# Head mixing with rows of exponentials sorted by DMA and 64x64 products

## The chip, the cores and the metric

The kernel runs on one core of a Trainium2 chip. The time is the device time of one execution, in microseconds (us). One core has five engines that run their own queues in order and meet at semaphores: TensorE (PE in the profile; PEld is its loading of weights), VectorE (DVE), ScalarE (ACT), GpSimd (POOL) and SyncE (SP), which here issues DMAs.

## The reference, cut to what matters

The program is a whole network (a convolution stage, fast-weight attention, a pattern layer, this attention, a layer of experts). The change is in the attention with mixed heads; there are 4 images of 1024 positions, 8 heads of 32 channels:

```python
attn = jnp.einsum('bhnd,bhmd->bhnm', q, k) * scale
attn = jax.nn.softmax(attn, axis=-1)
attn = jnp.einsum('gh,bhnm->bgnm', conv_w, attn) + conv_b[None, :, None, None]
mean = attn.mean(axis=(0, 2, 3), keepdims=True)
var = attn.var(axis=(0, 2, 3), keepdims=True)
attn = (attn - mean) * jax.lax.rsqrt(var + BN_EPS)
attn = attn * bn_gamma[None, :, None, None] + bn_beta[None, :, None, None]
out = jnp.einsum('bhnm,bhmd->bhnd', attn, v)
```

So for each query the 8 rows of probabilities (one per head, 1024 keys long) are replaced by 8 mixtures of them, whose sum and sum of squares over everything give the normalization, and the mixtures weigh the values.

## The kernel before, in words

`head_mixing_stage` works image by image (`b`, 4 of them). After the projections of an image (`project`, `value_sums`) it goes through 64 tiles of 16 queries. A tile is [128, 1024] float32: its 128 rows are 8 heads times 16 queries, its columns the keys. 8 tiles make a block (128 queries); `t` is a tile's place in its block and `u` the tile's parity, which picks one of two buffers. In the order of a tile's life:

- POOL `masked(i)` makes the masked queries `qd` of tile i; PE `scores(i)` multiplies them with the keys, as 8 products of 64 rows by 32 columns that run side by side, into two banks of PSUM (one pair of banks per parity).
- DVE `maxima(i)` takes the negative maximum of each row; ACT `exponentials(i)` writes `ex` to SBUF and the row sums; DVE `inverse(i)` inverts the sums; POOL `weights(i)` multiplies the constant `kron` (the mixing matrix spread over 16 queries) by the inverses, which gives the weights `mix`.
- PE `mixed(i)` multiplies `mix` (128 by 128) with the tile, two products of 512 columns, into banks 4 and 5. ACT `keep(i)` copies them to `Aq`, ACT `squares(i)` sums the squares, DVE `running(i)` sums the values.
- PE `turn(i)` transposes `Aq` in 8 pieces into banks 6 and 7, and DVE `evacuate(i)` copies these to `A`.
- Once per block PE `values` multiplies `A` with the values (64 products) into banks 6 and 7, and DVE `outputs` copies the result to `H`.

Nothing but the order in which the code is written decides the order on an engine. On PE a tile is `mixed(i)`, `turn(i-1)`, `scores(i+2)`; at t = 1 `values` stands between `mixed` and `scores`, and `turn` comes last. On DVE it is `maxima(i+1)`, `running(i-1)`, `inverse(i+1)`, `outputs` at t = 1, `evacuate(i-1)`. On ACT it is `squares(i-1)`, `exponentials(i+1)`, `keep(i)`. Before `mixed(i)` PE waits for the masked queries of tile i+2, for `exponentials(i)`, for the weights of tile i and for `keep(i-1)`. SP issues seven loads when the stage begins and nothing more in it.

Of the kernel before, what the change touches and what calls it, by code (L numbers as in the profile page):

```python
# [12 lines left out]
ALU = mybir.AluOpType  # L13
# [1638 lines left out]
def head_mixing_stage(k, H):  # L1652


    nc, d = k.nc, k.d
# [7 lines left out]
    with ExitStack() as ctx:  # L1663
# [6 lines left out]
        kron = sb("kron", [P, HEADS, QT_])  # L1670
# [4 lines left out]
        ex = sb("ex", [P, 2, HW])  # L1675
        nm = sb("nm", [P, 2]); rsum = sb("rsum", [P, 2]); rinv = sb("rinv", [P, 2])
        mix = sb("mix", [P, 2, HEADS * QT_])
# [10 lines left out]
        names = ("w kron hb q q_act q_dve k k_ev v v_ev vs vs_ev qd s nm ex rinv mix aq cp sq run t ac pv pv_ev "  # L1688
                 "tot var sd dch pch").split()
        (s_w, s_kron, s_hb, s_q, s_q_act, s_q_dve, s_k, s_k_ev, s_v, s_v_ev, s_vs, s_vs_ev, s_qd, s_s, s_nm, s_ex, s_rinv,  # L1690
         s_mix, s_aq, s_cp, s_sq, s_run, s_t, s_ac, s_pv, s_pv_ev, s_tot, s_var, s_sd, s_dch, s_pch) = (
# [4 lines left out]
        with nc.Block() as block:  # L1696
            @block.sync
            def _(sp):
                sp.dma_start(wq[:, :, :, :], d["hm_wq"]).then_inc(s_w, 16)
                sp.dma_start(w[:, :, :], d["hm_w"]).then_inc(s_w, 16)  # L1700
                sp.dma_start(wcol[:, :], d["hm_wcol"]).then_inc(s_w, 16)
                sp.dma_start(wrow[:, :, :], d["hm_wrow"]).then_inc(s_w, 16)
                sp.dma_start(qmask[:, :, :], d["hm_qmask"]).then_inc(s_w, 16)
                sp.dma_start(cbcol[:, :], d["hm_cbcol"]).then_inc(s_w, 16)
                sp.dma_start(lane[:, :, :], d["hm_lane"]).then_inc(s_w, 16)

            @block.gpsimd
            def _(pool):
                def masked(b, i, u):
                    pool.wait_ge(s_s, b * TI + i + 1)  # L1710
                    src = q[:, :, bass.ds(i * QT_, QT_)].unsqueeze(2).broadcast_to([P, NPAIR, 2, QT_])
                    pool.tensor_tensor(qd[:, u, :, :, :], src,  # L1712
                                       qmask[:, :, :].unsqueeze(1).broadcast_to([P, NPAIR, 2, QT_]),
                                       ALU.mult).then_inc(s_qd, 1)

                def weights(b, i, u):
                    pool.wait_ge(s_rinv, b * TI + i + 1)
                    pool.tensor_tensor(mix[:, u, :], kron[:, :, :].rearrange("p g n -> p (g n)"),  # L1718
                                       rinv[:, u:u + 1].broadcast_to([P, HEADS * QT_]), ALU.mult).then_inc(s_mix, 1)

                pool.wait_ge(s_w, 112)
                pool.wait_ge(s_kron, 1)
                k.credit(pool, s_s, 2)
                with pool.Fori(0, B) as b:
                    pool.wait_ge(s_v, b + 1)
                    pool.tensor_copy(hb[:, :, :], H[:, :, bass.ds(b * HW, HW)]).then_inc(s_hb, 1)
                    pool.wait_ge(s_q_act, b * 4 + 4)
                    pool.wait_ge(s_q_dve, b * 4 + 4)
                    masked(b, 0, 0)
                    masked(b, 1, 1)  # L1730
                    with pool.Fori(0, TI // 2 - 1) as j:
                        for u in range(2):
                            masked(b, j * 2 + u + 2, u)
                            weights(b, j * 2 + u, u)
                    for u in range(2):
                        weights(b, TI - 2 + u, u)

            @block.tensor
            def _(pe):
# [4 lines left out]
                with pe.Fori(0, B) as b:  # L1744
# [69 lines left out]
                    def values(n):  # L1814
                        pe.wait_ge(s_ac, b * TI + n * NQ + NQ)
                        for m in range(MT):
                            for o in range(CH):
                                for j in range(4):
                                    g = 4 * o + j
                                    mm = pe.matmul(bank[6 + o][32 * j:32 * j + 32, 0:QB], v[:, m, DH * g:DH * g + DH],  # L1820
                                                   A[:, m, g, :], start=(m == 0), stop=(m == MT - 1))
                        mm.then_inc(s_pv, 1)

                    def block_of_queries(n, first, last):

                        for t in range(NQ):
                            i = n * NQ + t
                            more = not (last and t >= NQ - 2)
                            mixed(i, t % 2, more)
                            if t == 0 and not first:  # L1830
                                turn(i - 1, 1)
                            if t == 1 and not first:
                                values(n - 1)
                            if t > 1:
                                turn(i - 1, (t - 1) % 2)
                            if more:
                                scores(i + 2, t % 2)
# [8 lines left out]
                    value_sums()  # L1846
                    block_of_queries(0, True, False)
# [13 lines left out]
            def _(act):  # L1861
                k.load_table(act, ACT.Exp)
                with act.Fori(0, B) as b:

                    def exponentials(i, u):
                        act.wait_ge(s_nm, b * TI + i + 1)
                        act.activation(ex[:, u, :], flat2(psum[:, 2 * u:2 * u + 2, :]), ACT.Exp,  # L1867
                                       bias=nm[:, u:u + 1], accum_out=rsum[:, u:u + 1]).then_inc(s_ex, 1)
# [22 lines left out]
                    keep(0, 0, fresh=True)  # L1891
                    squares(0, 0)
                    act.wait_ge(s_aq, b * TI + 1)
                    exponentials(2, 0)
                    keep(1, 1, fresh=True)
                    with act.Fori(1, TI // 2 - 1) as j:
                        for u in range(2):
                            i = j * 2 + u
                            squares(i - 1, 1 - u)
                            act.wait_ge(s_aq, b * TI + i)  # L1900
                            exponentials(i + 1, 1 - u)
                            keep(i, u)
                    squares(TI - 3, 1)
                    act.wait_ge(s_aq, b * TI + TI - 2)
                    exponentials(TI - 1, 1)
                    keep(TI - 2, 0)
                    squares(TI - 2, 0)
                    keep(TI - 1, 1)
# [5 lines left out]
            def _(dve):  # L1914
                own = Steps(dve, s_pch)
                dve.wait_ge(s_w, 112)
                dve.tensor_tensor(kron[:, :, :], k.const("mkron").rearrange("p (g n) -> p g n", g=HEADS),
                                  wcol[:, :].unsqueeze(2).broadcast_to([P, HEADS, QT_]), ALU.mult).then_inc(s_kron, 1)
                dve.memset(sums[:, :], 0.0).then_inc(s_run, 1)
                dve.wait_ge(s_run, 1)  # L1920
                with dve.Fori(0, B) as b:
# [28 lines left out]
                    def block_of_queries(n, first, last):  # L1950
                        for t in range(NQ):
                            i = n * NQ + t
                            more = not (last and t == NQ - 1)
# [4 lines left out]
                            if more:  # L1958
# [14 lines left out]
                    maxima(0, 0)  # L1973
                    dve.wait_ge(s_vs, b + 1)
# [466 lines left out]
def constants():  # L2441
# [9 lines left out]
        "mkron": (i % 16) == (j % 16),  # L2451
# [9 lines left out]
def layout(inputs):  # L2461
# [54 lines left out]
    out["hm_wcol"] = np.repeat(a["L3_attn_conv_w"].T, P // HEADS, 0)  # L2516
    out["hm_wrow"] = np.repeat(a["L3_attn_conv_w"], DH, 0).reshape(CH, P, HEADS).transpose(1, 0, 2)
    out["hm_qmask"] = np.repeat((np.arange(P)[:, None, None] % 64 // DH == np.arange(2)[None, :, None]), 16, 2).astype(np.float32)
    out["hm_cbcol"] = np.repeat(a["L3_attn_conv_b"], P // HEADS)[:, None]
    mine = np.arange(P)[:, None, None] // 16 == np.arange(CH)[None, :, None] * 4 + np.arange(P)[None, None, :] // DH  # L2520
# [28 lines left out]
```

## Time and profile before

| | |
|---|---|
| median of 3 runs | 4664.12 us (4653.84 to 4673.27) |
| the profiled execution, its own time | 4656.92 us |
| its span (first to last instruction) | 4654.9 us |
| busy share of the span | PE 84%, DVE 60%, ACT 47%, POOL 18% |
| the stage of the change, first to last mixing product | 2801.3 to 4064.1 us |

Busy shares are means over stages with different limits; what is asked of this profile is what one tile of the stage waits for. Starts in the rows are us from the span's start. The ends of matmuls are modelled, so where one operation follows another the distance of the starts is the safer number.

### The profile page before, as it was taken

To read this page: it belongs to the slowest core of one execution; us is meant where nothing else is said; L and a number is where in the kernel's file an instruction comes from. 1 tells how busy PE (TensorE), PEld (TensorE's weight loads), DVE (VectorE), ACT (ScalarE), POOL (GpSimd) and SP (SyncE) were. 2 spreads that over 40 slices of the span, in tenths; PEclk is the share of its full clock that TensorE was granted. 3 is DMA by queue.
4 is the path that set the end of the run, shared out by engine and by line. 5 is a ranking of instruction groups with operands and counts; after the bars stand their busy time and mean duration, and the time that the engine had idled before them with its cause. 6 is when DMAs were issued, how large, how long until landed. Compare 5 with 4: busy or idle time off the path is not lost. (4 is left out here: it accounts for less than half of the span.)

```text
span 4654.9 us, 156020 instructions
## 1 busy us (share of the span) xinstructions
PE 3895.6 (84%) x64268; PEld 2373.9 (51%) x64269; DVE 2777.9 (60%) x5395; ACT 2194.1 (47%) x4155; POOL 820.1 (18%) x2119
## 2 busy tenths in 40 slices
PE   3468999879789997678889659999999999975995
PEld 1236777534367775245555434544545445544763
DVE  3545666320356663578888648858858858843343
ACT  1124555221345552366666517747747747712221
POOL 0000000000000000255555401111111111105022
PEclk7779999889899998899999879999999999977997
DMA  1001111000011110100000000000000000025223
GB/s 49 0 17 43 48 50 50 25 18 0 15 44 48 51 48 24 44 1 1 1 1 1 0 11 1 0 1 1 0 1 0 0 1 0 1 88 190 65 90 103
DMA packets 84139, 131.60 MB, mean 28 GB/s; under 512 B 11216, under 2 KB 66800, under 8 KB 82928
## 3 DMA queue, kind: packets, MB, share of 16 engines
q1 hardware_dynamic: 77808, 112.19, 7.2%
q0 software_dynamic: 6144, 16.79, 1.1%
q8 instruction: 134, 2.20, 0.2%
q14 instruction: 53, 0.43, 0.0%
HBM read 70.21 MB, written 58.72 MB: 28 GB/s over the span
## 5 line engine op out<-in xcount | busy, mean ns | idle before, releaser
L1801 PE MATMUL psum<-hm_ex,hm_mix 128*128 128x512 f32 x1024 | 510.7, 622 | 42.1 <-ACT hm_Aq L1881 38.1
L1867 ACT ACTIVATE hm_ex<-psum,hm_nm 128x1024 f32<-128x1024 f32 x256 | 285.6, 1116 | 298.5 <-DVE hm_nm L1925 298.5
L1801 PEld LDWEIGHTS psum<-hm_ex,hm_mix 128*128 128x128 f32 x1024 | 175.6, 191 | 352.6 <-issue 344.9
L1940 DVE COPY hm_A<-psum 128x1024 f32<-128x1024 f32 x256 | 313.0, 1222 | 51.1 <-PE psum L1810 47.8
L1935 DVE TENSOR_SCALAR_CACHE_REDUCE hm_plus<-hm_Aq,hm_cbcol,hm_sums 128x1024 f32<-128x1024 f32 x256 | 340.6, 1331 | 0.0
L1925 DVE TENSOR_REDUCE hm_nm<-psum 128x1 f32<-128x1024 f32 x256 | 311.2, 1216 | 14.0 <-PE psum L1789 14.0
L1810 PEld LDWEIGHTS psum<-K,hm_Aq 128*128 128x128 f32 x2048 | 236.7, 140 | 150.0 <-issue 145.4
L1872 ACT ACTIVATE hm_junk<-hm_Aq 128x1024 f32<-128x1024 f32 x256 | 270.6, 1057 | 30.3
L1347 ACT ACTIVATE pt_signs<-pt_acts,pt_tb 128x1024 f32<-128x1024 f32 (+1 forms) x224 | 227.6, 1017 | 115.5 <-POOL pt_tb L1214 94.8
L1789 PE MATMUL psum<-hm_kt,hm_qd 64*32 64x512 f32 x4096 | 280.4, 606 | 0.0
L1810 PE MATMUL psum<-K,hm_Aq 128*128 128x128 f32 x2048 | 266.6, 273 | 5.7 <-DVE hm_A L1940 5.6
L1881 ACT ACTIVATE hm_Aq<-psum 128x1024 f32<-128x1024 f32 x256 | 259.7, 1014 | 11.3 <-PE psum L1801 11.3
L1261 PE MATMUL psum<-pt_w_proc,pt_keptT 128*128 128x512 f32 x512 | 226.8, 601 | 10.0 <-ACT pt_keptT L1332 10.0
L690 PE MATMUL psum<-fw_w,fw_stage 128*128 128x512 f32 (+1 forms) x512 | 211.6, 538 | 24.5 <-DMA fw_w<-in_slow 24.4
L2252 ACT ACTIVATE ex_ht<-psum,ex_b 128x128 f32<-128x128 f32 x320 | 91.5, 368 | 286.7 <-PE psum L2184 286.7
L1718 POOL TENSOR_TENSOR hm_mix<-hm_kron,hm_rinv 128x128 f32<-128x128 f32 x256 | 102.2, 399 | 664.4 <-DVE hm_rinv L1930 664.4
L1431 DVE TENSOR_SCALAR_CACHE_REDUCE pt_over<-pt_acts,pt_tb 128x1024 f32<-128x1024 f32 (+1 forms) x96 | 101.8, 1098 | 166.7 <-POOL pt_tb L1214 166.7
L1241 PE MATMUL psum<-K,pt_acts 128*128 128x128 f32 x640 | 101.5, 321 | 106.1 <-DVE pt_acts L1459 80.1
L1712 POOL TENSOR_TENSOR hm_qd<-hm_q,hm_qmask 128x128 f32<-128x128 f32 x256 | 116.1, 454 | 411.9 <-PE psum L1789 300.7
L670 POOL TENSOR_TENSOR fw_loff<-fw_bg,K 128x256 f32<-128x256 f32 x64 | 55.0, 860 | 675.6 <-DVEq L983 675.6
L1261 PEld LDWEIGHTS psum<-pt_w_proc,pt_keptT 128*128 128x128 f32 x512 | 97.6, 193 | 129.4 <-issue 129.4
L723 PE MATMUL psum<-fw_rk,fw_ntx 64*64 64x64 f32 x4096 | 155.2, 227 | 5.5 <-issue 4.9
(370 smaller groups left out, 7996.7 us busy)
## 6 DMA issues: line engine op xcount, KB each, us to landing
fw_late<-fw_away SPq DMA_DIRECT2D x64, 384.0 KB, 3.1
ex_rows_in<-ex_zero SPq DMA_DIRECT2D x2, 5120.0 KB, 24.5
ex_xs<-ex_rows_in SPq DMA_DIRECT2D x80, 128.0 KB, 2.0
ex_rows_out<-ex_ys SPq DMA_DIRECT2D x80, 128.0 KB, 1.7
fw_away<-fw_kk SPq DMA_DIRECT2D x64, 128.0 KB, 1.7
fw_away<-fw_tr SPq DMA_DIRECT2D x64, 128.0 KB, 1.7
fw_away<-fw_qm SPq DMA_DIRECT2D x64, 128.0 KB, 1.7
ex_w<-in_ex_w SPq DMA_DIRECT2D x2, 4096.0 KB, 22.2
```

Source lines behind the costliest of these rows:

```text
L690: mm = pe.matmul(bank[n][:, 0:hi - lo], stage[:, h, :], w[:, h, lo:hi], start=(h == 0), stop=(h == CH - 1))
L1261: mm = pe.matmul(bank[4 + u], keptT[:, c, u, :], w_proc[:, c, :], start=(c == 0), stop=(c == N_IN // P - 1))
L1347: act.activation(signs[:, u, 0:n], acts[:, lane(j), u, 0:n], ACT.Sign, bias=tb[:, lane(j), u, 0:1], accum_out=tb[:, lane(j), u, 1:2]).then ...
L1789: mm = pe.matmul(bank[2 * u + c][32 * pr:32 * pr + 32, :], qd[64 * c:64 * c + 64, u, pr, :, :].rearrange("p j n -> p (j n)"), kt[64 * c:64 ...
L1801: mm = pe.matmul(bank[4 + c], mix[:, u, :], ex[:, u, 512 * c:512 * c + 512], start=True, stop=True)
L1810: mm = pe.transpose(bank[6 + m // 4][:, P * (m % 4):P * (m % 4) + P], Aq[:, u, P * m:P * m + P], k.const("ident"))
L1867: act.activation(ex[:, u, :], flat2(psum[:, 2 * u:2 * u + 2, :]), ACT.Exp, bias=nm[:, u:u + 1], accum_out=rsum[:, u:u + 1]).then_inc(s_ex, 1)
L1872: act.activation(junk[:, :], Aq[:, u, :], ACT.Square, accum_out=ssq[:, bass.ds(b * TI + i, 1)]).then_inc(s_sq, 1)
L1881: act.activation(Aq[:, u, :], flat2(psum[:, 4:6, :]), ACT.Copy).then_inc(s_cp, 1)
L1925: dve.tensor_reduce(nm[:, u:u + 1], flat2(psum[:, 2 * u:2 * u + 2, :]), AX.X, ALU.max, negate=True).then_inc(s_nm, 1)
L1935: dve.tensor_scalar(plus[:, :], Aq[:, u, :], cbcol[:, :], sums[:, :], ALU.add, ALU.add, accum_out=sums[:, :]).then_inc(s_run, 1)
L1940: dve.tensor_copy(A[:, :, :, QT_ * t:QT_ * t + QT_], flat2(psum[:, 6:8, :]).rearrange("p (m g n) -> p m g n", m=MT, g=HEADS)).then_inc(s_a ...
```

## The change

Each tile of exponentials gets a second copy, `sorted`, whose rows are in another order. Row 16h+n of `ex` is head h, query n. SP waits for `exponentials(i)` and issues two DMAs from SBUF to SBUF: even rows of `ex` to partitions 0 to 63 of `sorted`, odd rows to 64 to 127. A row is 1025 elements long (4100 bytes), since the row sum is written behind the 1024 exponentials and travels with them. Now each half of the partitions holds 8 heads times 8 queries, no product crosses the halves, and `mixed` is four products of 64 rows by 64 columns by 512 instead of two of 128 by 128 by 512. `kron` and `mix` shrink to 64 columns. The output rows now mean another pair of head and query, so `evacuate`, `outputs` and `values` read and write in other patterns (the same numbers of instructions and elements), and constants are laid out anew.

The order around it moves too: scores are made three tiles ahead instead of two, maxima two ahead instead of one, and exponentials two ahead, behind `keep` instead of ahead of it. `inverse(i)` waits for the two DMAs of tile i.

```diff
-        ex = sb("ex", [P, 2, HW])
+        ex = sb("ex", [P, 2, PITCH]); sorted_ = sb("sorted", [P, 2, PITCH])
...
+                with sp.Fori(0, B * TI // 2) as j:
+                    for u in range(2):
+                        sp.wait_ge(s_ex, j * 2 + u + 1)
+                        for r in range(2):
+                            sp.dma_start(sorted_[64 * r:64 * r + 64, u, 0:HW + 1], ex[r:P:2, u, 0:HW + 1]
+                                         ).then_inc((s_mv0, s_mv1)[u], 16)
...
                         if more:
-                            pe.wait_ge(s_qd, b * TI + i + 3)
-                            pe.wait_ge(s_ex, b * TI + i + 1)
+                            pe.wait_ge(s_qd, b * TI + i + 4)
+                            pe.wait_ge(s_ex, b * TI + i + 2)
                         pe.wait_ge(s_mix, b * TI + i + 1)
                         pe.wait_ge(s_cp, b * TI + i + 1)
+                        pe.sem_inc(s_go, 1)
                         for c in range(2):
-                            mm = pe.matmul(bank[4 + c], mix[:, u, :], ex[:, u, 512 * c:512 * c + 512],
-                                           start=True, stop=True)
+                            for r in range(2):
+                                o = slice(64 * r, 64 * r + 64)
+                                mm = pe.matmul(bank[4 + r][64 * c:64 * c + 64, :], mix[o, u, :],
+                                               sorted_[o, u, 512 * c:512 * c + 512], start=True, stop=True)
...
-                                scores(i + 2, t % 2)
+                                scores(i + 3, (t + 1) % 2)
...
                     def inverse(i, u):
-                        dve.wait_ge(s_ex, b * TI + i + 1)
-                        dve.reciprocal(rinv[:, u:u + 1], rsum[:, u:u + 1]).then_inc(s_rinv, 1)
+                        dve.wait_ge((s_mv0, s_mv1)[u], b * (TI * 16) + (i * 16 + (32 - 16 * u)))
+                        dve.reciprocal(rinv[:, u:u + 1], sorted_[:, u, HW:HW + 1]).then_inc(s_rinv, 1)
...
-                        dve.tensor_copy(A[:, :, :, QT_ * t:QT_ * t + QT_],
-                                        flat2(psum[:, 6:8, :]).rearrange("p (m g n) -> p m g n", m=MT, g=HEADS)
-                                        ).then_inc(s_ac, 1)
+                        dve.tensor_copy(A[:, :, :, QT_ * t:QT_ * t + QT_].rearrange("p m g (r n) -> p r (m g) n", r=2),
+                                        psum[:, 6:8, :].rearrange("p r (a n) -> p r a n", n=HQ)).then_inc(s_ac, 1)
...
-                            if more:
-                                maxima(i + 1, (t + 1) % 2)
+                            if not (last and t >= NQ - 2):
+                                maxima(i + 2, t % 2)
```

On POOL, in the loop over pairs of tiles, the masked queries (`hm_qd`) of a tile stood ahead of the weights (`hm_mix`) for which the same product of PE waits. The loop before:

```order
L1731 ISA
L1712 ISA
L1712 TENSOR_TENSOR hm_qd<-hm_q,hm_qmask 128x128
L1717 ISA
L1718 TENSOR_TENSOR hm_mix<-hm_kron,hm_rinv 128x128
```

The same loop of the change:

```order
L1742 ISA
L1728 TENSOR_TENSOR hm_mix<-hm_kron,hm_rinv 128x64
L1720 ISA
L1722 ISA
L1722 TENSOR_TENSOR hm_qd<-hm_q,hm_qmask 128x128
```

The two have changed places: `weights(i)` comes first and is half as wide, `masked(i+3)` follows it, and `mixed(i)` waits for both.

On ACT, in the loop over pairs of tiles (`hm_junk` is `squares`, `hm_ex` the exponentials, `hm_Aq` is `keep`), before:

```order
L1872 ACTIVATE hm_junk,hm_ssq<-hm_Aq 128x1024
L1900 REGISTER_ALU
L1866 ISA
L1867 ACTIVATE hm_ex,hm_rsum<-psum,hm_nm 128x1024
L1876 REGISTER_ALU
L1878 REGISTER_ALU
L1881 ACTIVATE hm_Aq<-psum 128x1024
```

and in the change:

```order
L1892 ACTIVATE hm_junk,hm_ssq<-hm_Aq 128x1024
L1896 ISA
L1898 REGISTER_ALU
L1901 ACTIVATE hm_Aq<-psum 128x1024
L1886 ISA
L1887 ACTIVATE hm_ex<-psum,hm_nm 128x1024
```

`keep(i)` moved ahead of the exponentials, which now belong to tile i+2. On SP two DMAs per tile are new, after the stage's loads:

```order
L1710 ISA
L1714 DMA hm_sorted<-hm_ex 64x1025 x2
L1712 REGISTER_ALU
L1714 DMA hm_sorted<-hm_ex 64x1025 x2
L1710 REGISTER_ALU
```

That is a pair of tiles per turn of the loop, with nothing between the two DMAs of a tile.

## Rows read from the trace of the kernel before

**Rows 1.** The page, its first line.

```profile
span 4654.9 us, 156020 instructions
```

**Rows 2.** Windows, 100 us inside the stage: busy us per engine, granted clock.

```profile
3300.00:3400.00 100.00, 96.76 (x1022) 50.25 (x1021) 86.29 (x121) 73.91 (x114) 19.18 (x45) 1.00 0.00 0
```

**Rows 3.** Groups of the stage by line: busy, mean ns, idle before and releaser.

```profile
L1801 PE MATMUL psum<-hm_ex,hm_mix 128*128 128x512 f32 x1024 | 510.7, 622 | 42.1 <-ACT hm_Aq L1881 38.1 <-POOL hm_mix L1718 4.0
L1867 ACT ACTIVATE hm_ex<-psum,hm_nm 128x1024 f32<-128x1024 f32 x256 | 285.6, 1116 | 298.5 <-DVE hm_nm L1925 298.5
```

**Rows 4.** Timeline, one ordinary tile: start, duration, engine, line, operation.

```profile
3336.51 1.98 PE L1801 MATMUL psum<-hm_ex,hm_mix 128*128 128x512 f32 x4
...
3337.99 1.12 ACT L1867 ACTIVATE hm_ex<-psum,hm_nm 128x1024 f32<-128x1024 f32 x1 [0.42 <-DVE hm_nm L1925]
3338.34 1.04 PE L1810 MATMUL psum<-K,hm_Aq 128*128 128x128 f32 x8
...
3339.01 0.19 ACT L1867 ACTIVATION_READ_ACCUMULATOR hm_ex<-psum,hm_nm 128x1 f32 x1
3339.10 1.01 ACT L1881 ACTIVATE hm_Aq<-psum 128x1024 f32<-128x1024 f32 x1
...
3339.23 0.16 DVE L1930 RECIPROCAL hm_rinv<-hm_rsum 128x1 f32<-128x1 f32 x1
...
3339.30 1.09 PE L1789 MATMUL psum<-hm_kt,hm_qd 64*32 64x512 f32 x16
...
3339.47 0.40 POOL L1718 TENSOR_TENSOR hm_mix<-hm_kron,hm_rinv 128x128 f32<-128x128 f32 x1 [2.17 <-DVE hm_rinv L1930]
...
3340.32 1.98 PE L1801 MATMUL psum<-hm_ex,hm_mix 128*128 128x512 f32 x4
...
3340.65 0.45 POOL L1712 TENSOR_TENSOR hm_qd<-hm_q,hm_qmask 128x128 f32<-128x128 f32 x1 [0.78 <-PE psum L1789]
```

**Rows 5.** Timeline behind the values of a block.

```profile
3350.01 0.49 DVE L1947 COPY H<-psum 128x128 f32 x2 [3.00 <-PE psum L1820]
...
3351.84 1.22 DVE L1940 COPY hm_A<-psum 128x1024 f32<-128x1024 f32 x1 [1.34 <-PE psum L1810]
...
3352.98 1.21 DVE L1925 TENSOR_REDUCE hm_nm<-psum 128x1 f32<-128x1024 f32 x1
...
3355.34 1.01 ACT L1881 ACTIVATE hm_Aq<-psum 128x1024 f32<-128x1024 f32 x1
...
3355.71 0.40 POOL L1718 TENSOR_TENSOR hm_mix<-hm_kron,hm_rinv 128x128 f32<-128x128 f32 x1 [4.24 <-DVE hm_rinv L1930]
3356.23 0.45 POOL L1712 TENSOR_TENSOR hm_qd<-hm_q,hm_qmask 128x128 f32<-128x128 f32 x1
...
3356.49 1.96 PE L1801 MATMUL psum<-hm_ex,hm_mix 128*128 128x512 f32 x4 [1.08 <-ACT hm_Aq L1881]
3356.67 1.21 DVE L1925 TENSOR_REDUCE hm_nm<-psum 128x1 f32<-128x1024 f32 x1
```

**Rows 6.** Timeline of PE, the same place one block earlier.

```profile
3321.32 1.96 PE L1801 MATMUL psum<-hm_ex,hm_mix 128*128 128x512 f32 x4 [1.08 <-ACT hm_Aq L1881]
```

**Rows 7.** Timeline of SP, the stage's first two loads.

```profile
2753.75 0.33 SPq L1699 DMA_DIRECT2D hm_wq<-in_hm_wq  x1
2754.13 0.59 SPq L1700 DMA_DIRECT2D hm_w<-in_hm_w  x1
```

**Rows 8.** DMA issues: count, KB each, median us from issue to landing.

```profile
ex_xs<-ex_rows_in SPq DMA_DIRECT2D x80, 128.0 KB, 2.0
...
fw_away<-fw_tr SPq DMA_DIRECT2D x64, 128.0 KB, 1.7
...
hm_wq<-in_hm_wq SPq DMA_DIRECT2D x1, 512.0 KB, 3.8
hm_w<-in_hm_w SPq DMA_DIRECT2D x1, 512.0 KB, 4.1
...
ho_w<-in_hm_out SPq DMA_DIRECT2D x1, 256.0 KB, 2.6
```

More of the change, by code:

```diff
@@ L1687, in head_mixing_stage @@
         st = sb("st", [P, 8, CH]); toff = sb("toff", [P, CH, B])
[L1688 to L1691, printed above, removed]
+        names = ("w kron hb q q_act q_dve k k_ev v v_ev vs vs_ev qd s nm ex mv0 mv1 rinv mix aq cp sq run t ac pv pv_ev "
+                 "tot var sd go dch pch").split()
+        (s_w, s_kron, s_hb, s_q, s_q_act, s_q_dve, s_k, s_k_ev, s_v, s_v_ev, s_vs, s_vs_ev, s_qd, s_s, s_nm, s_ex, s_mv0, s_mv1, s_rinv,
+         s_mix, s_aq, s_cp, s_sq, s_run, s_t, s_ac, s_pv, s_pv_ev, s_tot, s_var, s_sd, s_go, s_dch, s_pch) = (
              k.sem(f"s_hm_{n}") for n in names)
@@ L1730, in _ @@
                     masked(b, 1, 1)
-                    with pool.Fori(0, TI // 2 - 1) as j:
+                    masked(b, 2, 0)
+                    with pool.Fori(0, TI // 2 - 2) as j:
                         for u in range(2):
-                            masked(b, j * 2 + u + 2, u)
                             weights(b, j * 2 + u, u)
-                    for u in range(2):
-                        weights(b, TI - 2 + u, u)
+                            masked(b, j * 2 + u + 3, 1 - u)
+                    weights(b, TI - 4, 0)
+                    masked(b, TI - 1, 1)
+                    for i in range(TI - 3, TI):
+                        weights(b, i, i % 2)
             @block.tensor
@@ L1827, in block_of_queries @@
                             i = n * NQ + t
-                            more = not (last and t >= NQ - 2)
+                            more = not (last and t >= NQ - 3)
                             mixed(i, t % 2, more)
@@ L1846, in _ @@
                     value_sums()
+                    pe.wait_ge(s_qd, b * TI + 3)
+                    pe.wait_ge(s_ex, b * TI + 1)
+                    pe.sem_inc(s_go, 1)
+                    scores(2, 0)
                     block_of_queries(0, True, False)
@@ L1891, in _ @@
                     keep(0, 0, fresh=True)
+                    exponentials(2, 0)
                     squares(0, 0)
-                    act.wait_ge(s_aq, b * TI + 1)
-                    exponentials(2, 0)
                     keep(1, 1, fresh=True)
+                    exponentials(3, 1)
                     with act.Fori(1, TI // 2 - 1) as j:
@@ L1899, in _ @@
                             squares(i - 1, 1 - u)
-                            act.wait_ge(s_aq, b * TI + i)
-                            exponentials(i + 1, 1 - u)
                             keep(i, u)
[L1903 to L1908, printed above, removed]
+                            exponentials(i + 2, u)
+                    for u in range(2):
+                        squares(TI - 3 + u, 1 - u)
+                        keep(TI - 2 + u, u)
                     squares(TI - 1, 1)
@@ L1952, in block_of_queries @@
                             i = n * NQ + t
-                            more = not (last and t == NQ - 1)
-                            if more:
-                                maxima(i + 1, (t + 1) % 2)
+                            if not (last and t >= NQ - 2):
+                                maxima(i + 2, t % 2)
                             if not (first and t == 0):
                                 running(i - 1, (t - 1) % 2)
-                            if more:
+                            if not (last and t == NQ - 1):
                                 inverse(i + 1, (t + 1) % 2)
@@ L1973, in _ @@
                     maxima(0, 0)
+                    maxima(1, 1)
                     dve.wait_ge(s_vs, b + 1)
@@ L2450, in constants @@
         "gn_avg": same(8) / 8.0,
-        "mkron": (i % 16) == (j % 16),
+        "mkron": (i % 8) == (j % 8),
         "one": np.ones((P, P)),
@@ L2515, in layout @@
     out["hm_wq"] = np.repeat(rows(a["L3_attn_w_qkv"][:, :C]).reshape(P, CH, 4, 1, 64), 2, 3).reshape(P, CH, 4, P)
[L2516 removed]
+    out["hm_wcol"] = np.tile(np.repeat(a["L3_attn_conv_w"].T, 8, 0), (2, 1))
     out["hm_wrow"] = np.repeat(a["L3_attn_conv_w"], DH, 0).reshape(CH, P, HEADS).transpose(1, 0, 2)
     out["hm_qmask"] = np.repeat((np.arange(P)[:, None, None] % 64 // DH == np.arange(2)[None, :, None]), 16, 2).astype(np.float32)
[L2519 to L2520 removed]
+    out["hm_cbcol"] = np.tile(np.repeat(a["L3_attn_conv_b"], 8), 2)[:, None]
+    mine = np.arange(P)[:, None, None] // 8 % 8 == np.arange(CH)[None, :, None] * 4 + np.arange(P)[None, None, :] // DH
     out["hm_lane"] = mine.astype(np.float32)
```

23 lines of the change are left out of this document (12 added, 11 removed).

## The prediction

> **What bounds the kernel now.** I read the page first for the size of things: 4654.9 us in all [rows 1]. Then the windows inside the stage: in 100 us PE is busy 96.76, DVE 86.29, ACT 73.91, at a granted clock of 1.00, the upper of its two levels, 2.4 GHz [rows 2]. That looks like a stage bound by PE, and the groups agree: the mixing products, which the change halves, are PE's largest item with 510.7 us and waited only 42.1 us, while ACT stands idle 298.5 us for DVE's maxima [rows 3].
>
> A mean over 100 us mixes two things, so I went on to the timeline. In an ordinary tile PE starts its product at 3336.51, the transposes at 3338.34, the scores at 3339.30 and the next product at 3340.32: 1.83 + 0.96 + 1.02 = 3.81 us, with no gap [rows 4]. But DVE is hardly less full. Where it does not wait for PE, its five instructions of a tile (maxima, sum of values and the reading of its sum, inverse, evacuation) take from 3352.98 to 3356.67, 3.69 us [rows 5]. So an ordinary tile has 0.12 us to give, whatever PE saves, and two tiles cannot take less than 7.38 us against 7.62 now.
>
> The rest is at the block's values. The same product, with the same wait of 1.08 us, starts at 3321.32 and at 3356.49 [rows 5, 6], so a block takes 35.17 us: six ordinary steps of 3.81 and two that hold the values, 35.17 - 22.86 = 12.31 us. There DVE waits 3.00 us for the values and 1.34 us for the transposes behind them [rows 5].
>
> **The change, part by part.** *The product.* Nothing before is 64 by 64 by 512. The nearest row is the scores: eight 64-row products of 512 columns side by side, 1.02 us from their start to the next operation's [rows 4]. I take 1.02 for the four new ones instead of 1.83: PE saves 0.81 us per tile. Bounds: 0.91 (half of 1.83) and 1.83 (no two side by side).
>
> *What this buys at the best.* On ordinary steps 0.12 us each, DVE's limit. At the values the product of tile t = 1 stands ahead of them on PE and everything behind follows it, so the two steps shrink by its 0.81.
>
> *What is new on the path.* Between exponentials and inverse there are now two DMAs, and each tile's product leads to the exponentials of the tile two later: `mixed(i)`, `keep(i)`, `exponentials(i+2)`, the DMAs, `inverse(i+2)`, `weights(i+2)`, `masked(i+5)` behind it on POOL, `mixed(i+2)`. This ring must close once in two tiles. Term by term, with L for the time from SP's first issue to the second landing:
> - product to the start of `keep`: 1.09, and 0.26 more by which POOL's start lies behind the modelled end of the scores (3340.65 against 3340.39) [rows 4]: 1.35. With the 0.03 by which DVE follows ACT it would be 1.12.
> - `keep` to `exponentials`, which stand right behind it: 1.01 less the overlap of 0.10 seen between ACT's neighbours (3339.01 + 0.19 against 3339.10) [rows 4]: 0.92.
> - exponentials to the read sum, 3337.99 to 3339.20: 1.21. To SP, 0.03 (DVE starts 0.03 after it) [rows 4].
> - landing to DVE 0.03; inverse to POOL's start, 3339.23 to 3339.47: 0.24 [rows 4].
> - weights: 0.40 for 128 columns [rows 4], 0.20 for 64; I take it as proportional (bounds 0.20 and 0.40).
> - masked queries: 0.45, and the 0.12 between 3356.11 and 3356.23 [rows 5]: 0.57. They stood ahead of the weights before, where they cost this path nothing.
> - POOL to PE: 0.14, as from `keep`'s end, 3356.35, to the product at 3356.49 [rows 5].
>
> The sum is 4.69 + L for two tiles. Before, no ring through a DMA existed. It is free if it is under 7.38, that is L under 2.69, and costs what PE's saving gave on ordinary steps at L = 2.93.
>
> *L.* No row shows a copy from SBUF to SBUF, so I bound it. The two DMAs move 128 x 4100 bytes = 524.8 kB (512.5 KB). The second issue starts 0.38 us behind the first [rows 7], while the first is still on its way. Low end: 256 KB land in 2.6 us, and the 1024 KB of the first two loads in 0.38 + 4.1 = 4.48 [rows 7, 8]; so 786 kB more took 1.88 us, 418 kB per us. 128 KB out of SBUF land in 1.7 [rows 8], of which 131/418 = 0.31 are the bytes, 1.39 the rest. 1.39 + 524.8/418 = 2.65. High end: 4.1 + 0.38 = 4.48, the second of two loads in a queue. The nearest row is the load of 512 KB in 128 rows of 4096 bytes, 3.8 us; it reads memory, and at 128 KB a copy that ends in SBUF (2.0) is 0.3 slower than one that starts there (1.7) [rows 8]. I take 3.8 - 0.3 = **3.5**.
>
> *What is queued behind the new wait.* On DVE `inverse(i+1)` waits for the landing, and `outputs`, `evacuate(i-1)` and the next `maxima` stand behind it. PE's transposes and ACT's exponentials wait for those. On SP nothing else is queued. What costs nothing: the other patterns of `evacuate` and `outputs` (same elements; if the pieces of 8 made a copy slower, it would show on DVE at once), 0.81 us less of PE (it turns into waiting).
>
> *The sum, per image* (63 steps between 64 products: three at the start, two at each of 7 sets of values, 46 ordinary ones, or 23 pairs):
> - pairs at 4.69 + 3.5 = 8.19 instead of 7.62: 0.57 each. The last two have no masked queries to wait for, 7.62, so 0. 21 x 0.57 = +12.0.
> - values: 7 x -0.81 = -5.7.
> - filling: the first product of an image comes later by L and by the masked queries less the narrower weights, 3.5 + 0.57 - 0.20 = +3.9.
> - the last product is shorter: -0.8.
>
> +9.4 per image, x 4 = **+38 us**. The profiled execution had 4656.92 us, of which 4654.9 is span; it would have 4695. The median of the runs is 7.2 us above it, 0.15%, and I put the sum on that: 4664 + 38 = **4702 us**. With other L the same sum is 4 x (21 x (L - 2.93) + 2 x (L - 3.50) + L + 0.37 - 6.5): zero at L = 3.1, and 24 x 4 = 96 us for each us of L. The bound of 0.5%, 23 us, about what a measurement can tell from no change here, lies at L = 2.9 and 3.35.
>
> **The rivals.** *The DMAs are hidden* (ends faster). At L = 2.65 the ring takes 7.34, under DVE's 7.38: 23 pairs x -0.24 - 5.7 + 3.0 - 0.8 = -9.0, x 4 = -36 us, 4628. For it: the transfer's bytes need 1.26 us at the rate of rows 7 and 8, no memory is read, and no other DMA runs (the windows show a share of 0.00 [rows 2]). Against: no row of 512 KB landed under 3.8. It decides below L = 2.9.
>
> *Half rate.* Each DMA writes 64 partitions only. If that halves the rate, the bytes take 2 x 1.26 = 2.51 and L = 3.90: pairs 8.59, 21 x 0.97 + 2 x 0.40 - 5.7 + 4.3 - 0.8 = 19.0, x 4 = +76 us, 4740. No row shows a copy into 64 partitions, so the traces speak neither for nor against; it lies between my bounds. The Trainium skill has this as a rule (SBUF — State Buffer, "Door 1: The DMA port swizzle" and "Can I just issue two DMAs to hit both halves?"): 64 partitions reach 8 of 16 ports, a copy into them was measured at 196 GB/s, and two copies to the two halves serialize. By that figure, an estimate, the bytes take 2.68 us, L is 4.07 and the time 4757; no run here shows it yet.
>
> *No net change.* L between 2.9 and 3.35 gives back on 46 steps what the 7 sets of values save.
>
> *PE is not faster.* If the four products run one pair after the other (1.83), 0.81 comes back on the ring and at the values: (21 + 2) x 0.81 + 5.7 = 24 us per image, +134 with the forecast, 4798. The scores, which do run side by side, speak against it. A clock that falls to 1.2 GHz because PE now waits would cost in the same way; the windows show 1.00 at 96.76 busy of 100 [rows 2], and nothing of a stage with PE at 3.0 of 4.1.
>
> **How the numbers follow.** The forecast, L from 3.35 to 3.7, 0.28; half rate, L above that, 0.24; hidden, 0.32; no net change, 0.13; PE not faster, 0.03. So faster by over 0.5% 0.32, within it 0.13, slower 0.55. The low end is the hidden case, 4628, with a little for a product of 0.91: 4625. The high end is near L = 4.48 (21 x 1.55 + 2 x 0.98 - 6.5 + 4.85 = 32.9, x 4 = +131, 4795): 4790. The likeliest case's own range (L 3.35 to 3.9) is 4687 to 4740.
>
> **What the profile after would show.** The DMA issues give L directly: about 3.1 us from the second issue to landing if I am right, 2.3 if hidden, 3.5 or more at half rate. The inverse should be the DVE instruction with the idle time, released by the DMA. Steps between products should alternate in sums of about 8.2 per two tiles with PE idle ahead of the product behind POOL's masked queries or weights; 7.4 with DVE gapless would mean hidden. The product's distance to the next operation should be 1.02. The forecast is wrong if L is under 2.9, if POOL's half-width weights and ACT's order shorten the ring by much more than I took, or if evacuation in pieces of 8 is slower, which would raise DVE's 3.69 itself.

## The result and the profile after

The changed kernel takes 4987.71 us (median of 4 runs, 4977.71 to 4993.21), the kernel before 4663.86 beside it (4 runs). The ratio is 1.0693, with a 95% interval of 1.0668 to 1.0717. The forecast was 4702 and the range ended at 4790: slower was right, but +324 us stand where +38 were predicted.

The profiled execution of the changed kernel, 4977.71 us. First the page: its first line, the four groups that tell most (busy us, mean ns, idle before and releaser), and the DMA issue (KB each, median us to landing).

```profile
span 4975.6 us, 159149 instructions
...
L1817 PE MATMUL psum<-hm_sorted,hm_mix 64*64 64x512 f32 x2048 | 323.8, 704 | 379.8 <-POOL hm_qd L1722 357.0
L1901 ACT ACTIVATE hm_Aq<-psum 128x1024 f32<-128x1024 f32 x256 | 262.4, 1025 | 639.7 <-PE psum L1817 639.7
...
L1956 DVE COPY hm_A<-psum 128x1024 f32<-128x1024 f32 x256 | 309.9, 1211 | 65.9 <-PE psum L1826 65.3
...
L1946 DVE RECIPROCAL hm_rinv<-hm_sorted 128x1 f32<-128x1 f32 x256 | 41.8, 163 | 408.0 <-DMA hm_sorted<-hm_ex 407.6
...
hm_sorted<-hm_ex SPq DMA_DIRECT2D x512, 256.2 KB, 5.3
```

Against [rows 3]: the mixing product shrank from 510.7 to 323.8 us of busy time, but its wait grew from 42.1 to 379.8. On DVE the inverse, an instruction of 0.16 us, waits 408 us for the copies. Evacuation in pieces of 8 costs nothing: 1211 ns, as before (1.22 in [rows 5]).

The windows: 100 us of the stage, as [rows 2], then two neighbouring blocks, each from the first product behind a set of values to the same product one block later, then a block that ran at a granted clock of 1.00 throughout (us; busy us of PE, PEld, DVE, ACT and POOL; granted clock, DMA share, GB/s).

```profile
3300.00:3400.00 100.00, 72.16 (x887) 33.75 (x875) 67.66 (x96) 57.40 (x92) 12.70 (x36) 0.90 0.59 94
3314.97:3358.39 43.42, 30.13 (x385) 14.09 (x385) 29.97 (x42) 25.36 (x40) 5.64 (x16) 0.96 0.61 97
3358.39:3404.96 46.57, 33.89 (x386) 15.72 (x385) 30.27 (x42) 25.36 (x40) 5.64 (x16) 0.85 0.60 92
3860.74:3904.12 43.38, 28.65 (x385) 13.60 (x384) 29.87 (x42) 25.36 (x40) 5.66 (x16) 1.00 0.61 97
```

A block took 35.17 us before. Of the three here two take 43.4 us, and the one with the lowest granted clock takes 46.57. The timeline shows the ring of the prediction closing, once for each parity of tile.

```profile
3404.96 1.09 PE L1817 MATMUL psum<-hm_sorted,hm_mix 64*64 64x512 f32 x8
...
3408.47 0.19 ACT L1887 ACTIVATION_READ_ACCUMULATOR hm_ex<-psum,hm_nm 128x1 f32 x1
...
3409.87 1.09 PE L1817 MATMUL psum<-hm_sorted,hm_mix 64*64 64x512 f32 x8 [1.35 <-POOL hm_qd L1722]
3410.89 1.09 PE L1826 MATMUL psum<-K,hm_Aq 128*128 128x128 f32 x8
...
3411.17 1.02 ACT L1901 ACTIVATE hm_Aq<-psum 128x1024 f32<-128x1024 f32 x1 [1.48 <-PE psum L1817]
...
3412.09 1.11 ACT L1887 ACTIVATE hm_ex<-psum,hm_nm 128x1024 f32<-128x1024 f32 x1
...
3413.09 0.20 ACT L1887 ACTIVATION_READ_ACCUMULATOR hm_ex<-psum,hm_nm 128x1 f32 x1
...
3414.56 0.16 DVE L1946 RECIPROCAL hm_rinv<-hm_sorted 128x1 f32<-128x1 f32 x1 [2.30 <-DMA hm_sorted<-hm_ex]
...
3415.83 1.23 PE L1817 MATMUL psum<-hm_sorted,hm_mix 64*64 64x512 f32 x8 [2.83 <-POOL hm_qd L1722]
3416.99 1.97 PE L1826 MATMUL psum<-K,hm_Aq 128*128 128x128 f32 x8
...
3418.89 1.64 PE L1802 MATMUL psum<-hm_kt,hm_qd 64*32 64x512 f32 x16
3419.18 0.17 DVE L1946 RECIPROCAL hm_rinv<-hm_sorted 128x1 f32<-128x1 f32 x1 [0.96 <-DMA hm_sorted<-hm_ex]
3419.43 0.29 POOL L1728 TENSOR_TENSOR hm_mix<-hm_kron,hm_rinv 128x64 f32<-128x64 f32 x1 [3.92 <-DVE hm_rinv L1946]
3419.68 0.46 POOL L1722 TENSOR_TENSOR hm_qd<-hm_q,hm_qmask 128x128 f32<-128x128 f32 x1
...
3420.47 1.09 PE L1817 MATMUL psum<-hm_sorted,hm_mix 64*64 64x512 f32 x8
```

From 3409.87 the ring runs: product to `keep` 1.30, to the exponentials 0.92, to the read sum 1.20 (3413.29), to the inverse 5.89, to the weights 0.25, to the masked queries 0.25, to the next product but one 0.79: 10.60 us. The other tile's copies take the same: 3408.66 to 3414.56, 5.90. Less 0.03 at each end, **L is 5.84 us**, where 3.5 was taken and 4.48 was the bound. One more thing is in these rows: behind PE's wait of 2.83 the transposes took 1.97 and the scores 1.64, against 1.09 each a tile earlier. There the granted clock is at its lower level, 1.2 GHz (from 3416 to 3420 its mean is 0.58); stretches like this one make the 0.85 of the second block.

### The profile page after: what moved, and what is told of

It is laid out like the page before. It is cut to its first block and busy times, and to the rows that moved or that the text cites. A ratio compares the mean times of both kernels' runs of the same rounds, so it can differ in the third digit from the quotient of the medians.

```text
span 4975.6 us, 159149 instructions
## 1 busy us (share of the span) xinstructions
PE 3859.1 (78%) x65292; PEld 2295.0 (46%) x65293; DVE 2762.4 (56%) x5395; ACT 2169.8 (44%) x4155; POOL 782.4 (16%) x2119
## 5 line engine op out<-in xcount | busy, mean ns | idle before, releaser
L1817 PE MATMUL psum<-hm_sorted,hm_mix 64*64 64x512 f32 x2048 | 323.8, 704 | 379.8 <-POOL hm_qd L1722 357.0
L1901 ACT ACTIVATE hm_Aq<-psum 128x1024 f32<-128x1024 f32 x256 | 262.4, 1025 | 639.7 <-PE psum L1817 639.7
L1826 PEld LDWEIGHTS psum<-K,hm_Aq 128*128 128x128 f32 x2048 | 268.8, 163 | 268.8 <-issue 236.6
L1826 PE MATMUL psum<-K,hm_Aq 128*128 128x128 f32 x2048 | 339.4, 319 | 24.3 <-DVE hm_A L1956 16.5
L1817 PEld LDWEIGHTS psum<-hm_sorted,hm_mix 64*64 64x64 f32 x2048 | 63.6, 145 | 616.0 <-issue 616.0
L1956 DVE COPY hm_A<-psum 128x1024 f32<-128x1024 f32 x256 | 309.9, 1211 | 65.9 <-PE psum L1826 65.3
L1802 PE MATMUL psum<-hm_kt,hm_qd 64*32 64x512 f32 x4096 | 321.3, 691 | 2.6 <-DVE hm_vsum L1990 2.6
L1728 POOL TENSOR_TENSOR hm_mix<-hm_kron,hm_rinv 128x64 f32<-128x64 f32 x256 | 75.4, 295 | 1271.4 <-DVE hm_rinv L1946 1271.4
L1946 DVE RECIPROCAL hm_rinv<-hm_sorted 128x1 f32<-128x1 f32 x256 | 41.8, 163 | 408.0 <-DMA hm_sorted<-hm_ex 407.6
```

The lines of the kernel that those rows point to most:

```text
L1802: mm = pe.matmul(bank[2 * u + c][32 * pr:32 * pr + 32, :], qd[64 * c:64 * c + 64, u, pr, :, :].rearrange("p j n -> p (j n)"), kt[64 * c:64 ...
L1817: mm = pe.matmul(bank[4 + r][64 * c:64 * c + 64, :], mix[o, u, :], sorted_[o, u, 512 * c:512 * c + 512], start=True, stop=True)
L1826: mm = pe.transpose(bank[6 + m // 4][:, P * (m % 4):P * (m % 4) + P], Aq[:, u, P * m:P * m + P], k.const("ident"))
L1901: act.activation(Aq[:, u, :], flat2(psum[:, 4:6, :]), ACT.Copy).then_inc(s_cp, 1)
L1956: dve.tensor_copy(A[:, :, :, QT_ * t:QT_ * t + QT_].rearrange("p m g (r n) -> p r (m g) n", r=2), psum[:, 6:8, :].rearrange("p r (a n) -> ...
```

## The experiments

The theory was that L alone makes the loss, through the ring of 4.69 + L. The rivals were: contention of the copies with the engines, any wait on a DMA, and the clock. All ratios are to the kernel before in the same comparison. The diffs are cut to the lines that matter; `...` marks what is left out of a line.

**The copies by themselves** (`p1_copies`). Eight repetitions of nine kinds of copies, in a stage put ahead of the program, each waited for before the next:

```diff
...
+elif n.startswith("halves"): moves = [(z[64*r:64*r+64, 0:m], a[64*r:64*r+64, 0:m]) for r in range(2)]
+elif n.startswith("alone"):  moves = [(z[0:64, 0:m], a[0:P:2, 0:m])]
+elif n.startswith("spread"): moves = [(z[r:P:2, 0:m], a[64*r:64*r+64, 0:m]) for r in range(2)]
+else:                        moves = [(z[64*r:64*r+64, 0:m], a[r:P:2, 0:m]) for r in range(2)]  # pair
```

> The kernel before with a stage put in ahead, on an idle core, in which SP issues nine kinds of copies from SBUF to SBUF, each kind eight times and each time waiting for it. In the changed kernel the two copies of a tile take 5.87 us from the first issue to the inverse. If that is the price of the copies themselves, the kind `pair` (the same rows, partitions and pitch) takes 5.7 to 5.9 here too; if it comes from sharing SBUF with four busy engines, clearly less, 3.5 to 4.5. If destinations of 64 partitions are what slows them, `one` (all 128 partitions in one copy, in the same order) takes 3.0 to 3.9 and `halves1024` as long as `pair1024`; if rows of 4100 bytes at a pitch of 4112 are, then `pair1024` (4096 bytes, pitch 4096) and `pairwide` (pitch 4352) are faster than `pair`, and `one1024` faster than `one`; if reading every second partition is, `halves1024` is faster than `pair1024`.

The timeline of SP: start, us from the first issue of a kind to the end of its last issue (not to its landing), copies. The sorting pairs of 1025 and of 1024 elements share a row, as do the single copies.

```profile
26.41 90.05 SPq L165 DMA_DIRECT2D pair_to<-pair_from  x32
121.25 42.59 SPq L165 DMA_DIRECT2D pairwide_to<-pairwide_from  x16
168.66 43.68 SPq L165 DMA_DIRECT2D one_to<-one_from  x16
215.18 31.34 SPq L165 DMA_DIRECT2D halves_to<-halves_from  x16
249.74 27.32 SPq L165 DMA_DIRECT2D alone_to<-alone_from  x8
280.43 29.72 SPq L165 DMA_DIRECT2D spread_to<-spread_from  x16
313.12 24.85 SPq L165 DMA_DIRECT2D half_to<-half_from  x16
```

From a kind's first issue to the first of the next kind lie all its repetitions, 16 or 8. So a repetition of the sorting pair takes (121.25 - 26.41) / 16 = 5.93 us, one copy of all 128 partitions 46.52 / 16 = 2.91, two copies of adjacent halves 34.56 / 8 = 4.32, adjacent source into every second partition 32.69 / 8 = 4.09, one copy of every second partition alone (half the bytes) 30.69 / 8 = 3.84. For the sorting pair with half the elements, the last kind, 7 repetitions lie between its first issue and its last two, which take 1.10: (24.85 - 1.10) / 7 = 3.39. So all of L is there on an idle core (5.93 against 5.84), and contention falls. So does the row length: the pair with rows 1088 elements apart took 47.41 / 8 = 5.93, and in the issues view (us from issue to landing) the length in bytes makes no difference:

```profile
pair_to<-pair_from SPq DMA_DIRECT2D x16, 256.2 KB, 4.8
...
one_to<-one_from SPq DMA_DIRECT2D x8, 512.5 KB, 2.9
...
pair_to<-pair_from SPq DMA_DIRECT2D x16, 256.0 KB, 4.8
one_to<-one_from SPq DMA_DIRECT2D x8, 512.0 KB, 2.9
```

Splitting a copy into halves costs 1.4 us, and reading every second partition into 64 adjacent ones costs 1.6 more. Why that reading is slow, these runs do not show.

**No copies** (`e1_no_copy`; the products read the exponentials unsorted, and the inverse waits for the exponentials alone; the result is not the attention's).

```diff
-mm = pe.matmul(..., mix[o, u, :], sorted_[o, u, 512 * c:512 * c + 512], ...)
+mm = pe.matmul(..., mix[o, u, :], ex[o, u, 512 * c:512 * c + 512], ...)
```

> The changed kernel without the copies: the four products read the exponentials where they are, so heads and queries are mixed in the wrong rows, and the inverse waits for the exponentials again. Ring theory (the change lost its time because the ring from one product to the product of the tile two later holds the copies; everything else in it is a gain): the ring is 4.69 us for two tiles, under DVE's 7.38, and the time is about 4628, 0.992 of before. Rival (the loss is on the engines: a clock of 1.2 GHz in part of the stage, evacuations in pieces of 8, four products instead of two): it stays above 4850.

4607.68 us, ratio 0.9868 (0.9845 to 0.9892): the whole loss hangs on the copies, and without them the change would gain 1.3%, 20 us more than the ring theory gave. Rows of PE and ACT show what limits a tile then:

```profile
3305.95 1.09 PE L1811 MATMUL psum<-hm_ex,hm_mix 64*64 64x512 f32 x8 [1.39 <-POOL hm_qd L1716]
...
3307.25 1.03 ACT L1895 ACTIVATE hm_Aq<-psum 128x1024 f32<-128x1024 f32 x1 [1.52 <-PE psum L1811]
...
3308.17 1.11 ACT L1881 ACTIVATE hm_ex<-psum,hm_nm 128x1024 f32<-128x1024 f32 x1
...
3309.17 0.20 ACT L1881 ACTIVATION_READ_ACCUMULATOR hm_ex<-psum,hm_nm 128x1 f32 x1
...
3309.61 0.66 PE L1811 MATMUL psum<-hm_ex,hm_mix 64*64 64x512 f32 x4 [0.53 <-ACT hm_ex L1881]
```

It is a second ring, which the prediction had not seen: product, `keep`, the exponentials two tiles on, and the *next* product, which waits for them ahead of itself: 1.30 + 0.92 + 1.20 + 0.24 = 3.66 us per tile (3305.95 to 3309.61).

**Half the elements** (`e3_half_bytes`; the first 512 columns are not copied, the products read ones there).

```diff
-sp.dma_start(sorted_[64 * r:64 * r + 64, u, 0:HW + 1], ex[r:P:2, u, 0:HW + 1] ...
+sp.dma_start(sorted_[64 * r:64 * r + 64, u, HW // 2:HW + 1], ex[r:P:2, u, HW // 2:HW + 1] ...
```

> The changed kernel with only the second half of each row (and its sum) copied, 513 elements instead of 1025; the products read ones in the first half, so the result is not the attention's. If the copies are bound by their bytes, they take 1.39 + 4.48/2 = 3.6 us, the ring 8.3 and the time about 4715; if by something fixed per copy, they stay above 5 us and the time above 4890.

4705.47 us, ratio 1.0079 (1.0055 to 1.0103). As expected where the cost goes with the bytes: 2.54 us less of L (5.93 to 3.39 on the idle core) gave back 282 us; 244 of them by the formula's 96 us for each us of L, and the clock rose with it (1.00 in the 100 us from 3300).

**One copy of all partitions** (`e4_one_copy`; as many bytes in one copy, unsorted; the result is not the attention's).

```diff
-for r in range(2):
-    sp.dma_start(sorted_[64 * r:64 * r + 64, u, 0:HW + 1], ex[r:P:2, u, 0:HW + 1] ...
+sp.dma_start(sorted_[:, u, 0:HW + 1], ex[:, u, 0:HW + 1] ...
```

> The changed kernel with one copy per tile, all 128 partitions of the exponentials to the same 128 partitions, in place of the two that sort (so the products mix the wrong queries). If the size of L, and in it the reading of every second partition into 64 adjacent ones, makes the loss: one such copy landed 2.9 us after its issue on an idle core, L is 3.2 to 3.5, and by the prediction's formula the time is 4670 to 4705 us. If any DMA in the ring costs this much, or the second wait itself, the time stays above 4900.

4659.44 us, ratio 0.9996 (0.9985 to 1.0007), even a little below what was expected. All the bytes through the ring in one copy cost 1.3% against no copies; the sorting pair costs 8%. So neither the bytes nor a DMA in the ring as such makes the loss. This run changes the number of copies and their pattern together; the copies by themselves part the two, 1.4 us and 1.6.

**Another pattern, same sorting** (`e7_spread4`).

```diff
-for r in range(2):
-    sp.dma_start(sorted_[64 * r:64 * r + 64, u, 0:HW + 1], ex[r:P:2, u, 0:HW + 1] ...
+for r in range(4):
+    sp.dma_start(sorted_[r:P:4, u, 0:HW + 1], ex[32 * r:32 * r + 32, u, 0:HW + 1] ...
```

> The same sorting by four copies of 32 adjacent source partitions each into every fourth partition of the destination, with the masked queries' columns ordered query by query so that the result is the same. If the slow part is the reading of every second partition, L is about 4.5 (three issue distances of 0.5, then a landing of some 2.7, then 0.3 to the inverse) and the time by the formula is 4740 to 4830 us. If any scattering across partitions is as slow as the changed kernel's, or four issues cost more than two, it is 4960 to 5050.

4819.6 us, ratio 1.0344 (1.0323 to 1.0364): half of the loss is gone with four copies instead of two, as expected where the pattern that is read is slow. Its timeline gives the ring a second point:

```profile
3331.62 1.09 PE L1817 MATMUL psum<-hm_sorted,hm_mix 64*64 64x512 f32 x8 [1.65 <-POOL hm_qd L1722]
...
3334.84 0.20 ACT L1887 ACTIVATION_READ_ACCUMULATOR hm_ex<-psum,hm_nm 128x1 f32 x1
...
3339.53 0.16 DVE L1946 RECIPROCAL hm_rinv<-hm_sorted 128x1 f32<-128x1 f32 x1 [1.10 <-DMA hm_sorted<-hm_ex]
...
3340.81 1.09 PE L1817 MATMUL psum<-hm_sorted,hm_mix 64*64 64x512 f32 x8 [1.63 <-POOL hm_qd L1722]
```

From the read sum (3335.04) to the inverse are 4.49 us, so L is 4.43; 4.69 + 4.43 = 9.12, and the pair of tiles takes 9.19.

**Masked queries ahead of the weights** (`e2_mask_first`).

```diff
-weights(b, j * 2 + u, u)
 masked(b, j * 2 + u + 3, 1 - u)
+weights(b, j * 2 + u, u)
```

> The changed kernel with POOL's order of before: the masked queries ahead of the weights for which the same product waits. Ring theory: 0.57 us less in each of about 21 pairs of tiles per image, so 48 us less, 4940. Rival (the masked queries are hidden, the wait on them in the profile is only the last of several that end together): within 0.5% of 4988.

4970.76 us, ratio 1.0642 (1.0616 to 1.0669): 17 us less than the changed kernel, not 48. The product now waits for the weights instead of the masked queries, and the stage ran at the lower clock more often: the product's mean grew from 704 to 747 ns, and the granted clock in the 100 us from 3300 is 0.86 instead of 0.90. That this ate the other 31 us is argued, not shown.

**The clock** (`e8_filler`, `e8b_filler`): products whose result is overwritten, on PE ahead of its wait for the weights; six per tile in the first, one and a half in the second.

```diff
+pe.matmul(bank[4], k.const("ident"), kt[:, 0, :], start=True, stop=True)
+pe.matmul(bank[5][:, 0:256], k.const("ident"), kt[:, 1, 0:256], start=True, stop=True)
 pe.wait_ge(s_mix, b * TI + i + 1)
```

> The changed kernel with six idle products per tile on PE, ahead of the waits for the weights, into the banks that the mixing product then overwrites: PE waits less, the ring is the same. If the 56 us that the ring formula leaves over at L = 5.87 are the clock's (1.2 GHz in parts of the stage), the clock stays near 1.00 and the time is 4915 to 4950 us, though PE does more work. If the rest lies elsewhere in the ring, the time is 4975 to 5030.

5786.73 us, far above both expectations. Such a product takes 0.92 us (half of the 1.83 of the two in [rows 4]), six of them 5.5, more than the wait that they were to fill, so this says nothing of the clock. The second is sized to the wait:

> The changed kernel with one and a half idle products per tile (512 and 256 columns, 1.37 us by the rate of the 128 by 128 product, within the 1.35 to 2.83 us that PE waits) in place of the six that took more than the whole wait. If the 56 us left over by the ring formula at L = 5.87 are the clock's, the granted clock stays near 1.00 in the stage and the time is 4915 to 4950 us. If they lie elsewhere in the ring, it is 4975 to 5030.

4962.31 us, ratio 1.064 (1.0622 to 1.0658). Windows of it, as above:

```profile
3300.00:3400.00 100.00, 90.79 (x944) 42.59 (x940) 68.33 (x96) 57.37 (x91) 12.69 (x36) 1.00 0.62 96
```

With PE kept busy the clock is 1.00, and the kernel is 25 us faster though PE does more. That is less than expected, since the extra products also lengthen a block:

```profile
3362.05:3406.09 44.04, 40.11 (x417) 18.94 (x416) 29.87 (x44) 25.24 (x40) 5.64 (x16) 1.00 0.61 95
```

44.04 us where the changed kernel's block at 1.00 took 43.42 (the mean of four such blocks): 0.62 more, 17 us in the 28 blocks of 4 images. The clock's share in the changed kernel is then about 25 + 17 = 42 us. Its own blocks say nearly the same: the 28 of the profiled execution are together 38 us longer than 28 times 43.42.

**The order alone** (`e6_order_only`): scores three ahead and POOL's new order, with the 128 by 128 products of before and no copies.

> The order part of the change alone: scores three ahead, exponentials and maxima two ahead, POOL's weights ahead of the masked queries, with the mixing products of 128 by 128 and no copies, as before. If the gain of the kernels without a late copy comes from the narrower products, PE's 3.81 us per tile stand here too and the time is 4640 to 4680 us. If the other order alone made that gain, it is 4590 to 4620.

4785.26 us, ratio 1.0256 (1.0239 to 1.0273): both theories fell. The timeline shows the second ring again, now with the wide product:

```profile
3401.68 1.96 PE L1809 MATMUL psum<-hm_ex,hm_mix 128*128 128x512 f32 x4 [0.65 <-ACT hm_ex L1879]
...
3403.82 1.02 ACT L1893 ACTIVATE hm_Aq<-psum 128x1024 f32<-128x1024 f32 x1 [1.35 <-DVE hm_plus L1943]
...
3404.74 1.11 ACT L1879 ACTIVATE hm_ex<-psum,hm_nm 128x1024 f32<-128x1024 f32 x1
...
3406.18 1.96 PE L1809 MATMUL psum<-hm_ex,hm_mix 128*128 128x512 f32 x4 [0.66 <-ACT hm_ex L1879]
```

2.14 + 0.92 + 1.44 = 4.50 us per tile instead of 3.81. (The row of `keep` names DVE, but its start is 0.31 behind the product's 1.83, as it is 0.28 behind the narrow one's 1.02 above: it waits for PE.) The narrow product shortens this very ring, to 3.66.

**The ring over three tiles** (`e10_deep`, `e9_deep_pair`): scores four ahead, exponentials three ahead, four buffers, masked queries first; with the four copies of above, and with the change's own two.

```diff
-ex = sb("ex", [P, 2, PITCH]); sorted_ = sb("sorted", [P, 2, PITCH])
+ex = sb("ex", [P, 4, PITCH]); sorted_ = sb("sorted", [P, 4, PITCH])
-scores(i + 3, (t + 1) % 2)
+scores(i + 4, t % 2)
-maxima(i + 2, t % 2)
+maxima(i + 3, (t + 1) % 2)
-exponentials(i + 2, u)
+exponentials(i + 3, (u + 3) % 4)
```

> The four copies of the kernel just above, but scores four tiles ahead, maxima and exponentials three tiles ahead, four buffers each for the exponentials and the sorted rows, and the masked queries ahead of the weights: the ring then closes once in three tiles, (4.69 - 0.57 + 4.5) / 3 = 2.9 us per tile, under the 3.66 that a tile takes without any copy. If the loss is this ring alone, the time is that of the kernel without copies plus the filling, 4600 to 4640 us, below the kernel before, with the product computed in full. If the copies also cost by their traffic (queue, memory port, engines slowed), it is above 4664.

4594.15 us, ratio 0.9855 (0.9838 to 0.9871), the fastest kernel of this study and 6 us under the range of the first theory. The group of its inverse:

```profile
L1958 DVE RECIPROCAL hm_rinv<-hm_sorted 128x1 f32<-128x1 f32 x256 | 39.9, 156 | 0.4 <-DMA hm_sorted<-hm_ex 0.4
```

The copies are wholly hidden, though each of the four still lands 2.6 us after its issue, as in the kernel with the ring over two tiles.

> The change's own two copies of every second partition, in the deeper order of the kernel with four copies (scores four ahead, exponentials three ahead, four buffers, masked queries first). The copies take as long as in the changed kernel, L = 5.87, but the ring is shared by three tiles: (4.69 - 0.57 + 5.87) / 3 = 3.33 us per tile, under the 3.66 of a tile without copies. If only the ring's latency made the loss, the time is 4600 to 4650 us. If the copies' throughput counts too (their packets run for 3.4 us of each tile), copies of neighbouring tiles get into each other's way, L grows and the time is above 4700.

4655.31 us, ratio 0.9978 (0.9968 to 0.9988), between the two expectations. L grew, as the second theory had it: an issue lands after 6.1 us (5.3 in the changed kernel), at a DMA share of 0.91 in the 100 us from 3300. With so little idle time on the DMA engines the rate of these copies, and no longer the ring's terms, seems to set the pace (first the issue, with KB and median us to landing, then the timeline):

```profile
hm_sorted<-hm_ex SPq DMA_DIRECT2D x512, 256.2 KB, 6.1
...
3403.49 1.09 PE L1816 MATMUL psum<-hm_sorted,hm_mix 64*64 64x512 f32 x8 [1.47 <-POOL hm_mix L1728]
...
3406.55 0.16 DVE L1958 RECIPROCAL hm_rinv<-hm_sorted 128x1 f32<-128x1 f32 x1 [1.20 <-DMA hm_sorted<-hm_ex]
...
3407.23 1.09 PE L1816 MATMUL psum<-hm_sorted,hm_mix 64*64 64x512 f32 x8 [1.62 <-POOL hm_mix L1728]
...
3410.29 0.16 DVE L1958 RECIPROCAL hm_rinv<-hm_sorted 128x1 f32<-128x1 f32 x1 [1.20 <-DMA hm_sorted<-hm_ex]
```

3.74 us from landing to landing and from product to product, just over the 3.66 of a tile without copies.

## Why the prediction was wrong

**The step that failed is the term L**, taken as 3.5 and bounded at 4.48. The bound was the second of two loads that each fill 128 partitions. No row before showed a copy that reads every second partition into 64 adjacent ones, and its price is outside what 128-partition rows can bound: 5.93 us against 2.91 for the same bytes. For one copy of 128 partitions the 3.5 would even have been too much. The range stopped at 4790, a little below the 4795 that its own bound gave. At L = 5.84 the formula gives 4 x (21 x 2.91 + 2 x 2.34 + 5.84 + 0.37 - 6.5) = +262 us of the +324.

**The half-rate rival** pointed the right way and was also too small: 3.90 by rows, where adjacent halves now measure 4.32 and the sorting pair 5.93. The Trainium skill's rule that two copies to the two halves serialize (SBUF — State Buffer, "Can I just issue two DMAs to hit both halves?") agrees with the halves' 4.32 against 2.91 in direction; the estimate from its figure, 4.07, does not cover the pair. The rule was read for where a copy writes; neither it nor the prediction gave a chance to the pattern that is read.

**The clock** was priced as part of a rival of 0.03. It is the home of most of the rest. A block at L = 5.84 should take 35.17 + 3 x (10.53 - 7.62) - 0.81 = 43.09 us; the four that ran at 1.00 took 43.42 in the mean, the one at 0.85 took 46.57. Of the 62 us left over some 40 are the clock's, by the filler and by the blocks, and the 0.33 of 28 blocks make 9; the last dozen stays open.

**What held:** the ring, 4.69 + L = 10.53 against 10.60 for a pair, and 9.12 against 9.19 with four copies; the product's 1.02 to the next operation (3409.87 to 3410.89); the inverse as the waiting instruction on DVE; evacuation at no cost. The weights took 295 ns, not 0.20, but the masked queries start 0.25 behind them. In part the terms cancelled: POOL to PE took 0.33 (3420.14 to 3420.47), not 0.14, while weights and masked queries together took 0.71, not 0.77, and the terms up to the read sum 3.42, not 3.48.

**What was seen for the wrong reason:** the floor of an ordinary tile. DVE's 3.69 was named; without copies the second ring ends it at 3.66. The two are so near that the sum did not suffer, which is luck, but the same ring makes the new order by itself cost 2.6%, which the prediction counted as free.

Not tried: one copy that sorts all 128 partitions at once, the narrow products in the old order, and the wait for the exponentials behind the product instead of ahead of it, which would open the second ring.

## What to carry to other kernels

When a change puts a transfer on a ring, write the ring as "terms + L over n tiles" and ask first how many tiles it spans: four sorting copies lost 3.4% over two tiles and gained 1.5% over three (with the masked queries first), and the change's own two went from a loss of 6.9% to none. Bound the price of a copy only by rows with its own partition pattern; where there is none, the upper end is open, and a range that ends at a convenient row is too short. Price an order change without its companion too: here the order alone lost 2.6%, and with narrow products and no copies it gained 1.3%.

## What the runs showed of the hardware

Copies from SBUF to SBUF of 512 KB in all, on an idle core, per repetition: 2.91 us as one copy of 128 partitions, 4.32 as two adjacent halves, 4.09 from adjacent halves into every second partition, 5.93 from every second partition into adjacent halves. So scattering was cheap on the writing side and dear on the reading side. Rows of 4096 or 4100 bytes made no difference. In the changed kernel PE fell to the lower clock level during or behind some of its waits of 2.4 to 4.1 us (not at those of 2.82 and 2.80 that ended at 3325.83 and 3336.41), and the loss of clock came on top of the waits that caused it. With four copies, where the ordinary waits from 3313 on are 1.29 to 1.65, and without copies, where they are mostly 0.53, the granted clock of the 100 us from 3300 is 1.00.
